# Statistics of four images run ahead, image 0 loaded by tiles, and tiles of image 1 between the squares

## The reference

```python
# first block
y = depthwise_conv_7x7(x) + dw_b                          # NCHW, then to NHWC
mu, var = mean(y, -1), mean(square(y - mu), -1)           # over the 96 channels
y = (y - mu) * rsqrt(var + 1e-6) * ln_w + ln_b
y = gelu(y @ w1 + b1)                                     # 96 -> 384
gx = sqrt(sum(square(y), (H, W)))                         # per image and channel
nx = gx / (mean(gx, -1) + 1e-6)
y = grn_gamma * (y * nx) + grn_beta + y
z = x + (y @ w2 + b2)                                     # 384 -> 96
# second block
zq = clip(floor(z * 2**16) / 2**16, -2**15, 2**15 - 1)
out = depthwise_conv_3x3(zq, power_of_two(w)) + floor_fixed(b)
```

## Time and profile before

| | us |
|---|---|
| median of 3 runs | 1006.76 |
| lowest, highest | 1004.44, 1007.73 |
| the profiled execution, its time | 1008.35 |
| its span, first to last instruction | 1006.2 |
| PE busy, share of the span | 939.4, 93% |
| DVE busy | 806.6, 80% |
| ACT busy | 756.5, 75% |
| POOL busy | 415.7, 41% |
| mean granted TensorE clock | 0.963 |

### The profile page before, as it was taken

The page is one execution under the profiler, slowest core; times in us unless marked ns, Lnnn a source line. Parts: engine busy times, 40 slices in busy tenths (PEclk is TensorE's granted clock), DMA queues, the critical chain, the costliest instruction groups (busy, mean ns, idle before and its releaser), DMA issues.

```text
span 1006.2 us, 22653 instructions
## 1 busy us (share of the span) xinstructions
PE 939.4 (93%) x6342; PEld 694.5 (69%) x6342; DVE 806.6 (80%) x1429; ACT 756.5 (75%) x1331; POOL 415.7 (41%) x357
## 2 busy tenths in 40 slices
PE   5799999999999179999999999999999985999997
PEld 4688888888888166666666666666666643877775
DVE  5688888888888487988888888888888785888876
ACT  3588888888887277789988888899888841666664
POOL 2577777777776164333332333323333100111110
PEclk9799999999999677999999999999999996999999
DMA  7566676777662592655555555555553235899996
GB/s 202 126 206 206 207 208 205 212 209 215 207 204 96 155 249 60 186 150 171 175 167 166 165 169 159 162 172 165 180 166 111 82 107 161 257 310 311 312 309 213
DMA packets 110260, 188.47 MB, mean 187 GB/s; under 512 B 17357, under 2 KB 104036, under 8 KB 107268
## 3 DMA queue, kind: packets, MB, share of 16 engines
q1 hardware_dynamic: 99988, 173.55, 57.9%
q10 hardware_dynamic: 10240, 14.53, 4.8%
HBM read 129.77 MB, written 58.25 MB: 187 GB/s over the span
## 4 chain that ended last, share of the span: by engine, by line
PE 76%; SPq 8%; DMA 5%; DVE 4%; issue 3%; ACT 2%; POOL 1%; ACTq 0%; DVEq 0%; POOLq 0%
PE psum L664 27%; PE psum L743 23%; PE psum L733 6%; PE psum L734 6%; PE psum L735 6%; SPq L371 4%; PE psum L686 4%; PE psum L636 3%; SPq L366 2%; SPq L383 1%; DMA arena_r<-y_scratch 1%; DMA arena<-lines_a 1%; ACT arena L860 1%; DMA arena<-z_scratch 1%; DMA arena_r<-stats_scratch 1%
## 5 line engine op out<-in xcount | busy, mean ns | idle before, releaser
L664 PE MATMUL psum<-arena_r 112*128 112x464 f32 x1536 | 362.1, 386 | 12.2 <-DVE arena_r L997 5.7
L664 PEld LDWEIGHTS psum<-arena_r 112*128 112x128 f32 x1536 | 285.6, 191 | 59.2 <-issue 10.1
L743 PE MATMUL psum<-arena,w2s 128*96 128x448 f32 x672 | 266.6, 541 | 2.8 <-DVE w2s L1109 2.8
L893 ACT ACTIVATE arena<-psum,b1g 128x448 f32<-128x448 f32 x336 | 202.4, 630 | 59.4 <-PE psum L735 59.4
L568 POOL TENSOR_TENSOR arena_r<-arena,arena_r 96x448 fp32r<-96x448 f32 x112 | 136.7, 1220 | 264.7 <-DVE arena_r L1070 238.5
L743 PEld LDWEIGHTS psum<-arena,w2s 128*96 128x96 f32 x672 | 109.8, 164 | 119.4 <-issue 112.0
L733 PE MATMUL psum<-arena_r,w1h 96*128 96x448 f32 x336 | 153.6, 457 | 14.9 <-POOL arena_r L568 14.9
L803 ACT ACTIVATE arena<-psum,bias_a 64x112 f32<-64x112 f32 (+1 forms) x288 | 107.6, 407 | 60.5 <-PE psum L664 58.9
L557 POOL TENSOR_TENSOR arena<-arena 128x448 f32<-128x448 f32 x96 | 111.2, 1158 | 84.0 <-DVE arena L1025 84.0
L791 ACT ACTIVATE arena_r<-psum 112x448 fp32r<-112x448 f32 x192 | 93.4, 541 | 61.5 <-PE psum L636 61.5
L860 ACT ACTIVATE arena<-arena 128x1792 bf16<-128x1792 f32 (+1 forms) x91 | 136.8, 1503 | 2.7
(11 more groups left out here) (100 smaller groups left out, 1043.1 us busy)
## 6 DMA issues: line engine op xcount, KB each, us to landing
arena<-in_x_dram SPq DMA_DIRECT2D x95, 224.0 KB, 5.0
arena<-lines_a SPq DMA_DIRECT2D x46, 448.0 KB
arena<-z_scratch SPq DMA_DIRECT2D x87, 224.0 KB, 4.7
y_scratch<-arena SPq DMA_DIRECT2D x96, 196.0 KB, 4.9
arena<-in_x_dram SPq DMA_DIRECT2D x112, 168.0 KB, 2.6
z_scratch<-arena SPq DMA_DIRECT2D x112, 168.0 KB, 2.0
arena_r<-y_scratch SPq DMA_DIRECT2D x98, 168.0 KB, 2.6
arena_r<-stats_scratch SPq DMA_DIRECT2D x98, 168.0 KB, 3.1
```

Of the source, the lines that this page charges most:

```text
L664: mm = nc.tensor.matmul(p_conv[s % 2][:, 0:NCOL], w[:, p, s, TW * k:TW * k + TW], v[:, p, s, slot0 + k:slot0 + k + JP, :].rearrange("p j i ...
L743: mm = nc.tensor.matmul(p_o[k][0:C, 0:CH], w2s[:, p, m, :], hid[p][:, m, CH * t:CH * t + CH], start=(m == 0), stop=(m == MT - 1))
L893: nc.scalar.activation(hid[p][:, m, CH * t:CH * t + CH], p_h[m][:, 0:CH], ACT.Gelu, bias=b1g[:, m:m + 1]).then_inc(gelu_done, 1)
```

## The change

Six things, all between the first stage and the first `down`.

1. The statistics are made in two parts: images 0 to 3 first, the other twelve behind them. The last channel's mean is not updated any more, and its squares, POOL's last addition and the variance become DVE operations on the columns of a part (`last_square`, `one_over`, `of_images`). ACT sorts and takes from PSUM what belongs to the twelve. ACT loads the table of the root before the last channel's copy and that of Gelu behind the second root, each with a tiny activation. The last `back` goes to other PSUM banks, so that it does not wait for ACT's copy of the one before.
2. Image 0's factors are loaded in seven tiles (ACT's queue), image 0's y in seven tiles, and image 1's y and factors in seven tiles each (SP's queue, behind the end of the statistics' first store).
3. `store_lines` for the third stage's tables moves from behind the first stage into it; the twelve images' statistics are stored by SP behind the loads of x of image 0.
4. 18 and 32 matmuls without use (`keep_warm`) stand around PE's turn of the first part.
5. In DVE's head step tile 1 of image 1 comes ahead of the squares, and tile 2 between them; one of the three long squares goes to ACT, behind its last Gelu of image 0. POOL's power comes one tile later.
6. `FIRST_LEAD` is gone: in step 1 `down` runs two tiles behind `up`, not three.

```diff
-FIRST_LEAD = 3
+WARM = (18, 32)
...
-        res1 = conv(IG * NPAIR, G * PAIR)
+        res1 = arena[0:IG * NPAIR, ARENA - G * PAIR:ARENA]
...
-        p_stat = psum[:, 0:2, :]
+        p_stat = psum[:, 6:8, :]
...
+        def of_images(v, n0, n1):
+
+            return v.rearrange("p (q x) -> p q x", q=RP)[:, :, NRUN * n0:NRUN * n1]
...
-            return isinstance(i, int) and (i == 0 and (part == 0 or m == 0) or i == NIMG - 1 and part == 1 and m == 0)
+            return isinstance(i, int) and (i == 0 and (m < 2 if part == 0 else m == 0) or i == NIMG - 1 and part == 1 and m == 0)
...
-            load_y(0, 0)
-            sp.wait_ge(r_in[0], 16)
-            load_y(1, 1)
+            for t in range(NCH):
+                load_y(0, 0, t)
+            sp.wait_ge(stat_out, 16)
+            for t in range(NCH):
+                load_y(1, 1, t)
+                load_r(1, 1, t)
             for t in range(NCH):
                 load_x(0, t)
+            sp.wait_ge(stat_rows, 2)
+            sp.dma_start(*stat_rows_of(1, G)).then_inc(stat_out, 16)
             for t in range(NCH):
                 load_next(2, 0, t)
+            sp.wait_ge(stat_out, 32)
...
+            pe.wait_ge(b1_made, 1)
+            keep_warm(WARM[0])
+            pe.wait_ge(stat_in, 1)
+            turn_stats(0, 1)
+            keep_warm(WARM[1])
+            pe.wait_ge(stat_in, 2)
+            turn_stats(1, G)
             pe.wait_ge(stages["a"]["out"], 2 * NBATCH)
...
+            act.dma_start(*stat_rows_of(0, 1)).then_inc(stat_out, 16)
+            act.wait_ge(var_ready, 2)
+            nc.scalar.activation(of_images(root, IG, NIMG), of_images(var, IG, NIMG), ACT.Sqrt).then_inc(root_ready, 1)
+            nc.scalar.activation(gnx[:, :], halves[:, :], ACT.Gelu)
             act.wait_ge(stat_out, 16)
...
+            for t in range(NCH):
+                act.dma_start(rb[:, 0, CH * t:CH * t + CH], r_tile(0, t)).then_inc(t_in[0][t], 16)
+            act.wait_ge(rstd_made, 1)
...
+            dve.wait_ge(m2_done, C - 1)
+            last_square(0, IG)
             dve.wait_ge(root_ready, 1)
...
+            link(one_over(0, IG))
+            for to, v in in_order(0, IG):
+                ins = dve.tensor_copy(to, v)
+            ins.then_inc(stat_in, 1)
+            last_square(IG, NIMG)
             dve.wait_ge(stat_t, 1)
...
+            dve.tensor_copy(*stat_images(0, 1)).then_inc(stat_rows, 1)
+            dve.wait_ge(root_ready, 2)
+            one_over(IG, NIMG).then_inc(rstd_made, 1)
...
                     normalise(1, 1, 0)
-                    for m in range(MT):
-                        squares(0, 0, m, 0)
                     normalise(1, 1, 1)
+                    squares(0, 0, 0, 0)
+                    squares(0, 0, 1, 0)
+                    normalise(1, 1, 2)
                     squares(0, 0, 0, 1)
                     grn_sums(0, 0)
-                    normalise(1, 1, 2)
```

More of the change, by code:

```diff
@@ L554, in add @@
                             table_low(b + 1, q, 1 - p)
+                    if last and k == 2 * CB - 1:
+                        return
                     pool.wait_ge(wel, 3 * n + 3)
@@ L573, in step @@
                 for t in range(NCH):
-                    if t == (2 if fixed and i == 0 else NCH - 1) and not (fixed and i == NIMG):
+                    if t == (3 if fixed and i == 0 else NCH - 1) and not (fixed and i == NIMG):
                         pool.wait_ge(ss_ready, i + 1)
@@ L675, in back_waits, with back @@
                     evicted(pe, S, b, 2 * u + 1)
-                    need(pe, S["out"], 2 * b + u + 1 - len(outs))
-                def back(b, u, p):
+                    if not (S is stages["a"] and isinstance(b, int) and (b, u) == (NBATCH - 1, 1)):
+                        need(pe, S["out"], 2 * b + u + 1 - len(outs))
+                def back(b, u, p, to=None):
+                    to = outs[u % len(outs)] if to is None else to
                     for k in range(2):
@@ L749, in step @@
                 head, tail = fixed and i == 0, fixed and i == NIMG
-                lead = FIRST_LEAD if fixed and i == 1 else LEAD
-                for t in range(NCH + lead):
+                for t in range(NCH + LEAD):
                     if t < NCH and not tail:
@@ L758, in step @@
                         nc.tensor.matmul(p_grn[1 - p], ones[:, :], gx[:, :], start=True, stop=True).then_inc(gsum_done, 1)
-                    if t >= lead and not head:
-                        down(i - 1, 1 - p, t - lead)
+                    if t >= LEAD and not head:
+                        down(i - 1, 1 - p, t - LEAD)
             steps(pe, step)
@@ L837, in body @@
                                         table_high(b + 1, q, 1 - p)
+                            if rows_too and last and p == 1 and s == CB - 1:
+                                nc.scalar.activation(gnx[:, :], halves[:, :], ACT.Sqrt)
                             if rows_too or s < CB - 1:
@@ new lines, in one_over @@
+            def one_over(n0, n1):
+                r, q, v, to = [of_images(v, n0, n1) for v in (root, dsq[:, 0, :], var, rstd)]
+                link(dve.reciprocal(to, r))
+                link(dve.tensor_tensor(q, to, to, ALU.mult))
+                link(dve.tensor_tensor(q, q, v, ALU.mult))
+                link(dve.tensor_scalar(q, q, -0.5, 1.5, ALU.mult, ALU.add))
+                return dve.tensor_tensor(to, to, q, ALU.mult)
+            dve.wait_ge(m2_done, C - 1)
+            last_square(0, IG)
```

114 lines of the change are left out of this document (57 added, 57 removed).

## The result

| | before | after |
|---|---|---|
| median of 4 runs each, us | 1006.95 | 997.21 |
| lowest, highest | 1004.44, 1007.73 | 995.27, 998.14 |
| ratio to before, 95% interval | 1 | 0.9905 [0.9882, 0.9928] |
| profiled execution, its span | 1008.35, 1006.2 | 998.14, 996.3 |

The forecast was 996.0 (992.5 to 1001.5). So the gain is 7 to 10 us, and the two intervals share 0.9901 to 0.9928.

What follows compares the result with a forecast made beforehand. PE bounds the steady MLP; between first stage and steady state, latencies and half clock do. Terms gained 11.3 us, less a 0.6 stall: 1008.35 - 10.7 = 997.6 profiled, 996.0 against the median 1006.76; range 992.5 to 1001.5.

Steps and rivals of the forecast that it cites:

- Statistics: End of first stage: statistics of images 0 to 3 stored at 337.1 instead of 343.21 us, bounds 336.3 to 338.2.
- Memory: Statistics' store to first product: old 5.9 us plus 0.8 (bounds 0 to 3); product at 343.8, PE's first `up` at 346.2.
- Loads in each other's way: Rival, chance 0.10: image 0's factors share DMA engines with image 1's 14 tiles; gain 4 to 8, 999 to 1003 us.
- The clock over image 0: Image 0's tiles: clock fallen by 346.2, back 4.7 us later; eight tiles take 15.0 us plus 2.3 lost.
- The clock holds: Rival, chance 0.15: warm matmuls keep 2.4 GHz up to image 0; 2.4 us earlier, 993.6 us.
- The second hole: Behind image 1's tile 0: hole stays, 4.7 us, ended by ScalarE's Gelu instead of POOL's tile; PE resumes about 368.2.
- PE has no further wait, so the clock rises 4.7 us after 368.2: Behind the second hole: full clock back at 372.9 us instead of near 388.
- The residual's stall: Second `down` after the compared point: waits 0.6 us for tile 0's residual, lowering the gain from 11.3 to 10.7.
- A late sum: Rival, chance 0.20: VectorE's squares or POOL's root slip some 4 us, hole behind tile 1; 2.5 us less gained, 998.5 us.
- Signs of being wrong: Clock 0.50 well behind 375, first product after 346, VectorE ending the second hole, or a third stage of different length.
- the summed case: Main case between the stages, chance 0.48: all terms summed, 10.7 us gained; own range 993.5 to 998 us.
- Slower: Rival, chance 0.03: clock stays at half through the start; same point at about 391, 1.4 us later; 1012 us with one pair.

Runs made afterwards that it cites:

- e5: Changed kernel, but SP issues image 1's 14 tiles only once image 0's tile 0 (y and factors) has landed; 997.77 us, 0.9920 of the kernel before.
- e6: Changed kernel with image 1's tiles and image 0's y tiles 1 to 6 held back until tile 0 has landed; 998.17 us, 0.9917 of the kernel before.
- e1: Changed kernel plus 26 unused matmuls on PE ahead of image 1's tile 1, in the second hole; 995.07 us, 0.9883 of the kernel before.
- e4: Changed kernel without its own 18 and 32 unused matmuls; 996.22 us, 0.9906 of the kernel before.
- e7: Changed kernel with new statistics and loads, but squares, image 1's tile 1 and lead of three as before; 998.40 us, 0.9920 of the kernel before.
- e12: The changed kernel run once more, unchanged; 997.68 us against 1004.63 for the kernel before, ratio 0.9916.
- e2: Changed kernel with 58 unused matmuls instead of 32 ahead of image 0, and 10 behind the turned statistics; 996.35 us, 0.9901 of the kernel before.
- e3: Changed kernel with unused matmuls added in both holes, ahead of image 0 and of image 1's tile 1; 993.24 us, 0.9870 of the kernel before.
- e11: Changed kernel, both holes filled with unused matmuls; y tiles 0 to 2 load first, the rest once tile 0's factors land; 991.30 us, 0.9863 of before.

## Why the prediction was right, and where its steps were not

**Statistics: right.** The store stands 7.5 us behind the copy for a forecast 7.9. The rows estimated from 96 and 448 columns held: the reciprocal of 112 columns took 0.85 us (0.9 said). The table load of 1.28 us lies ahead of the copy, and the copy starts 0.02 us behind the tiny activation. The drain of 1.38 us that the Trainium skill (ScalarE: Activation LUTs, What ACT_TABLE_LOAD costs) adds does not show here either: 326.61 + 1.28 = 327.89, and the activation starts at 327.90; ahead of the load, the activation before it ends at 326.59.

**Memory: the term was mis-sized.** I had put "3.45" plus "0.8" from the load's issue to the product, between 0 and 3 more. It was 6.12, thus 2.7 more; `e5` and `e6` give 0.8 of it to image 1's tiles, the ones that I had blamed in the rival *Loads in each other's way*, and the rest to image 0's own y tiles, which had no price of their own in the 0.8. The six turns for the other twelve images, which stand ahead of the first `up`, came at 344.70, near the 345 said; ScalarE's copies for them could start only behind its seven load issues, which took 4.74 us. From product to `up` it took half a microsecond more (2.92 for 2.37): POOL's low part of the first tile took 1.58 us, while VectorE already worked on the second, and 1.12 before. With the statistics 0.4 early, PE's first `up` was 2.2 us late.

```profile
345.58 1.58 POOL L605 TENSOR_TENSOR arena_r<-arena,arena_r 96x448 fp32r<-96x448 f32 x1 [15.81 <-DVE arena_r L1130]
```

**The clock over image 0: right.** I had said that it falls and returns 4.7 us after PE's start; it returned after 4.6 (5.2 to 5.9 in `e1`, `e4`, `e5`, `e7` and `e12`). The rival *The clock holds* was wrong for the kernel as changed, and its price was about right: `e2`, which holds it there, gains 2.1 us against after and 3.3 against `e12`, for a forecast 2.4.

**The second hole: right.** 4.79 us for 4.7, ended by ScalarE's Gelu in place of POOL. Its start and its end were 1.7 us late with the load.

**The step that failed** is "PE has no further wait, so the clock rises 4.7 us after 368.2". PE had no further wait, and the clock rose 10.3 us after its return, 6.5 behind the sum over channels. Over all kernels in which it fell there it took 7.5 to 15.1 us from the return. The forecast counted from PE's return. Both lengths that its 4.7 came from (4.8 us behind 355.8, 3.9 behind 384.06) had been counted from the end of a wait, the last one ahead of the clock's return; counted so, the second hole agrees with the first, if the sum of 3 columns is taken for an interruption too, which is likely and not settled. This cost 2.6 us. With the 1.8 of the loads it makes the 4.4 us between 49.2 and 53.6.

**The residual's stall** of 0.6 us did not come: the residual started at 382.95, when PE was still in the `down` before. Where PE is earlier it comes, 0.49 to 0.52 us long, in `e1`, `e3` and `e11`. In `e11`:

```profile
377.70 2.50 PE L799 MATMUL psum<-arena,w2s 128*96 128x448 f32 x6 [0.51 <-DVE psum L1182]
```

**The sum** of 10.7 us was thus 7.2 in the stretch that it was made for. That the time came out so near the forecast (997.21 for 996.0) is in part luck: the profiled spans differ by 9.9 us only with the scatter of the first and third stages (1.1 and 1.6 us), and in the control `e12` the medians differ by 7.0. The rival *A late sum* had a near total, but its mechanism, squares or a root that slip, did not happen.

**Signs of being wrong.** Two of those that the forecast names did show: a clock of 0.50 well behind 375 (until 379.2), which is the step above, and a third stage of another length, which the scatter of the other profiles covers.

**Sums of the forecast that don't hold as they stand.** 51 intervals in 10.41 us are 0.204 us each, so 1.84 us for a tile and not 1.87; the eight tiles took 16.8 us for a forecast 17.3, which is why tile 0 ends only 1.7 us late. The bounds of store (336.3 to 338.2) and load (0 to 3) give the summed case 994.4 to 999.3 us, not 993.5 to 998. ScalarE's terms add up to 368.4, not 368.2. The terms of the rival *Slower* add up to about 392.7, not 391. Of these only the first and the third touch the total, by 0.3 us and 0.2 us.

What stays open beside it: in the same hole of the same program the clock fell 4.9 us behind PE's last matmul in after (364.1 to 369.0) and 1.5 behind it in `e12` (365.8 to 367.3). In the other kernels it was between the two. I found no event in the rows that tells them apart.

## What to carry to other kernels

Between two dense stages add up the chain engine by engine as here, but give the half clock behind a hole its own term, and count it from the last interruption of PE, not from its return: it was 4.6 us behind one hole and 10.3 behind the next, where a sum of 3 columns stood in between. If a hole can't be closed, fill it to its end with matmuls that nobody reads; filled halfway they brought nothing (after against `e4`), filled to the end 4.9 us (`e3`). When a small load is the head of a chain, issue beside it only what the next step needs, and the rest when it has landed: holding back everything moved the wait to the next load (`e6`), holding back nothing cost 3 us at the first one (after). The order of `e11` avoids both by the profile; its worth in the time is not shown apart.

## What the runs showed of the hardware

A load of 168 KB whose rows were read from memory and broadcast took 2.89 us to its user in `e6`, where the other queue was held back, 3.95 with three loads of that size there (`e11`), 5.30 with seven (`e5`), and 6.12 with the seven and those of image 1 that followed, of which eight were issued by then (after). In all four, six more such loads followed on its own queue.

The low stretches of the clock behind a hole were 6.8, 10.2 to 10.3, 13.6 to 13.7, 17.1, 20.5 and 27.3 us long. I had expected the clock to come back a fixed time behind PE's return; it took from 4.6 to 15.1 us. Behind PE's last wait of 0.6 us or more, or last matmul of 3 columns, it took 3.6 to 6.9 us, in all 22 cases.

POOL's operation on a tile of 96x448 took 1.12 us where VectorE stood still beside it for the most part (before, and `e5`) and 1.58 where VectorE worked on the next tile (after).
